# Two modulated linears around a 16-head per-token attention: softmax spreads ahead of the key turn, one key copy on ScalarE, stores a period later, another order in the fill

## The reference, cut to what matters

```python
def modulated_linear(x, s, aff_w, aff_b, w, b):
    style = s @ aff_w.T + aff_b
    w_mod = w[None, :, :] * style[:, None, :]
    demod = jax.lax.rsqrt(jnp.sum(w_mod * w_mod, axis=2) + EPS)
    ...
    return jnp.einsum('bni,boi->bno', x, w_mod) + b
...
x = x + L0(x)                       # modulated linear, clipped to +-256
kx = modulated_linear(x, ..., k_w)  # (B, N, 16 heads, 32)
scores = einsum('bnhd,bnjd->bnhj', kx, kx) / sqrt(32)
out = einsum('bnhj,bnjd->bnhd', softmax(scores), kx)
x = x + modulated_linear(out, ..., o_w)
```

## Time and profile before

| | us |
|---|---|
| median of 3 runs (760.2 to 765.8) | 765.31 |
| the profiled execution | 764.73 |
| its span in the profile | 762.9 |
| PE busy | 693.0 |
| DVE busy | 626.1 |
| ACT busy | 517.5 |
| POOL busy | 151.7 |

### The profile page before, as it was taken

How to read it: one execution, slowest core, us unless ns; L and a number is a source line. 1 busy time by engine, 2 the same in 40 slices (tenths; PEclk the granted TensorE clock), 3 DMA queues, 4 the chain that set the end, 5 groups by cost and what they waited for, 6 DMA issues and landing times.

```text
span 762.9 us, 21634 instructions
## 1 busy us (share of the span) xinstructions
PE 693.0 (91%) x8886; PEld 675.9 (89%) x8886; DVE 626.1 (82%) x1048; ACT 517.5 (68%) x1040; POOL 151.7 (20%) x139
## 2 busy tenths in 40 slices
PE   7999968999999999999999999999999899989896
PEld 6999968899888889988889998898999898889785
DVE  3689866998888898888899888889988888997662
ACT  4887855777667677666767766677767677765662
POOL 2024202222012222201222210222221122222200
PEclk9999999999999999999999999999999999989898
DMA  9267676467756676876567775657677665756853
GB/s 292 96 167 194 190 199 194 138 172 218 198 149 186 191 215 172 220 183 172 173 196 197 191 222 153 188 174 208 182 202 206 162 192 171 217 140 149 228 151 110
DMA packets 229666, 140.37 MB, mean 184 GB/s; under 512 B 141248, under 2 KB 223168, under 8 KB 229568
## 3 DMA queue, kind: packets, MB, share of 16 engines
q1 hardware_dynamic: 229568, 139.00, 65.0%
HBM read 71.85 MB, written 67.11 MB: 182 GB/s over the span
## 4 chain that ended last, share of the span: by engine, by line
DVE 53%; PE 22%; issue 9%; ACT 9%; DMA 4%; POOL 1%; SPq 1%; DVEq 0%; ACTq 0%; POOLq 0%
DVE p_bd L795 14%; PE y_ps L476 8%; PE lin_ps L413 7%; PE s_ps L458 6%; DVE o L773 5%; DVE x L754 5%; DVE v L744 4%; DVE x_lo L676 4%; DVE sc L759 3%; DVE x L752 3%; DVE sc L782 3%; DVE mx L764 3%; DVE p_turned L788 2%; DVE sc L766 2%; ACT sc L569 2%
## 5 line engine op out<-in xcount | busy, mean ns | idle before, releaser
L413 PE MATMUL lin_ps<-x_hi,w_hi 128*128 128x256 f32 x1008 | 287.3, 285 | 6.5 <-DVE w_lo L705 3.4
L413 PE MATMUL lin_ps<-x_lo,w_hi 128*128 128x256 f32 x1008 | 283.1, 281 | 0.0
L413 PE MATMUL lin_ps<-x_hi,w_lo 128*128 128x256 f32 x1008 | 282.9, 281 | 0.0
L383 POOL COPY k_bd<-k_rhs 32x1024 f32<-32x1024 f32 x128 | 147.4, 1151 | 568.1 <-DVE k_rhs L733 562.5
L413 PEld LDWEIGHTS lin_ps<-x_hi,w_hi 128*128 128x128 f32 x1008 | 191.3, 190 | 13.7 <-issue 13.5
L413 PEld LDWEIGHTS lin_ps<-x_lo,w_hi 128*128 128x128 f32 x1008 | 191.4, 190 | 0.2 <-issue 0.2
L413 PEld LDWEIGHTS lin_ps<-x_hi,w_lo 128*128 128x128 f32 x1008 | 191.3, 190 | 0.0
L413 PE MATMUL lin_ps<-y_hi,w_hi 128*128 128x256 f32 x528 | 150.4, 285 | 7.2 <-DVE y_lo L676 7.2
L413 PE MATMUL lin_ps<-y_lo,w_hi 128*128 128x256 f32 x528 | 149.3, 283 | 0.0
L413 PE MATMUL lin_ps<-y_hi,w_lo 128*128 128x256 f32 x528 | 149.2, 283 | 0.0
L509 ACT ACTIVATE x_hi<-x,style 128x256 fp32r<-128x256 f32 x252 | 113.0, 501 | 45.7 <-DVE x L754 39.4
(11 more groups left out here) (60 smaller groups left out, 727.1 us busy)
## 6 DMA issues: line engine op xcount, KB each, us to landing
x<-xT SPq DMA_DIRECT2D x32, 512.0 KB, 6.1
k_turned<-kx SPq DMA_DIRECT2D x32, 512.0 KB, 4.9
k_st<-k_turned SPq DMA_DIRECT2D x128, 128.0 KB, 3.1
v_turned<-k_rhs SPq DMA_DIRECT2D x32, 512.0 KB, 6.1
k_v<-v_turned SPq DMA_DIRECT2D x128, 128.0 KB, 3.2
y_turned<-y SPq DMA_DIRECT2D x128, 128.0 KB, 3.0
yr<-y_turned SPq DMA_DIRECT2D x32, 512.0 KB, 5.3
outT<-o SPq DMA_DIRECT2D x31, 512.0 KB, 4.0
```

The lines of the kernel that those rows point to most:

```text
L383: pool.tensor_copy(k_bd[HD * r:HD * (r + 1), r], k_rhs[HD * r:HD * (r + 1)]).then_inc(g_kbd, 1)
L413: mm = pe.matmul(lin_ps[:, n % NLB, 0:T], w[:, k, m * P:(m + 1) * P], r[:, k, :], start=(q == 0), stop=(q == len(passes) - 1))
```

## The change

On DVE in each period `spread_probabilities` comes ahead of `turn_k`, `turn_v` follows directly, and both `finish` come after `x_lo_of` of the next tile. POOL makes three of the four copies to `k_bd`; a new step `copy_keys` makes the fourth on ACT, behind `spread_some`. On SP `v_from_dram` is ahead of `y_to_dram`, and `store` is that of one tile earlier and stands between `y_to_dram` and `y_from_dram`. In the fill `scores` come sooner, `pv` later and in the middle of linears, with lists of ACT, DVE and SP to match. `WARM_L0` becomes 24. In the drain the lists get `copy_keys`, and the spreads of tile last-3 are ahead of the key turn of last-2.

```diff
-    WARM_STYLES, WARM_L0 = 9, 10
+    WARM_STYLES, WARM_L0 = 9, 24
+    POOL_GROUPS = 3
...
-            + blocks(K, 2) + blocks(L0, 4) + one("pv", 0) + one("scores", 1) + blocks(K, 3) + blocks(L0, 5)
-            + one("pv", 1) + one("scores", 2) + blocks(O, 0) + blocks(K, 4) + one("pv", 2) + one("scores", 3)
-            + blocks(O, 1) + blocks(K, 5) + one("pv", 3) + one("scores", 4))
+            + blocks(K, 2) + blocks(L0, 4) + one("scores", 1) + blocks(K, 3, [0, 1]) + one("pv", 0)
+            + blocks(K, 3, [2, 3]) + blocks(L0, 5, [0, 1]) + one("scores", 2) + blocks(L0, 5, [2, 3]) + one("pv", 1)
+            + blocks(K, 4) + one("scores", 3) + blocks(O, 0, [0, 1]) + one("pv", 2) + blocks(O, 0, [2, 3])
+            + blocks(K, 5) + one("scores", 4) + blocks(O, 1, [0, 1]) + one("pv", 3) + blocks(O, 1, [2, 3]))
...
             for i in range(FIRST_LOOP, last - 1):
                 k_to_dram(i - 1)
                 k_from_dram(i - 1)
+                v_from_dram(i - 2)
                 y_to_dram(i - 3)
-                v_from_dram(i - 2)
+                store(i - 5, 0, 1)
                 y_from_dram(i - 3)
                 load_x(i + 2)
                 v_to_dram(i - 1)
-                store(i - 4, 0, 1)
...
-                for r in range(R):
+                for r in range(POOL_GROUPS):
                     pool.tensor_copy(k_bd[HD * r:HD * (r + 1), r], k_rhs[HD * r:HD * (r + 1)]).then_inc(g_kbd, 1)
...
+            def copy_keys(c):
+                if c == 0:
+                    act.wait_ge(g_zero, 1)
+                act.wait_ge(v_krhs, c + 1)
+                for r in range(POOL_GROUPS, R):
+                    act.activation(k_bd[HD * r:HD * (r + 1), r], k_rhs[HD * r:HD * (r + 1)], ACT.Copy).then_inc(a_kbd, 1)
...
-                    (c0, x1_lo_of, 0), (c0, x1_lo_of, 1), (c1, turn_k), (c2, spread_probabilities), (c4, finish, 0),
-                    (c2, turn_v), (c4, finish, 1), (i + 1, x_lo_of, 0), (i + 1, x_lo_of, 1), (c3, y_lo_of, 0),
+                    (c0, x1_lo_of, 0), (c0, x1_lo_of, 1), (c2, spread_probabilities), (c1, turn_k), (c2, turn_v),
+                    (i + 1, x_lo_of, 0), (i + 1, x_lo_of, 1), (c4, finish, 0), (c4, finish, 1), (c3, y_lo_of, 0),
```

More of the change, by code:

```diff
@@ L305, in _ @@
             k_to_dram(2)
+            v_from_dram(1)
             k_from_dram(2)
-            v_from_dram(1)
             load_x(6)
             y_to_dram(0)
-            y_from_dram(0)
             v_to_dram(2)
             k_to_dram(3)
+            y_from_dram(0)
             k_from_dram(3)
@@ L316, in _ @@
             y_to_dram(1)
+            v_to_dram(3)
+            k_to_dram(4)
             y_from_dram(1)
-            v_to_dram(3)
-            store(0, 0, 1)
-            k_to_dram(4)
             k_from_dram(4)
@@ L323, in _ @@
             y_to_dram(2)
+            v_to_dram(4)
             y_from_dram(2)
-            v_to_dram(4)
-            store(1, 0, 1)
+            store(0, 0, 1)
             for i in range(FIRST_LOOP, last - 1):
@@ L334, in _ @@
                 v_to_dram(i - 1)
-                store(i - 4, 0, 1)
             k_to_dram(last - 2)
             k_from_dram(last - 2)
+            v_from_dram(last - 3)
             y_to_dram(last - 4)
-            v_from_dram(last - 3)
+            store(last - 6, 0, 1)
             y_from_dram(last - 4)
@@ L628, in _ @@
[L628 to L632, removed]
@@ L638, in _ @@
[L638 to L641, removed]
+                (1, k_out, 3), (O, roots), (2, x1_hi_of, 0), (2, x1_hi_of, 1), (0, copy_keys), (3, l0_out, 0),
+                (3, l0_out, 1), (3, l0_out, 2), (3, l0_out, 3), (4, x_hi_of, 0), (4, x_hi_of, 1), (0, even_scores),
@@ new lines, in _ @@
+                (2, k_out, 0), (0, exponentials), (2, k_out, 1), (2, k_out, 2), (2, k_out, 3), (1, copy_keys),
+                (3, x1_hi_of, 0), (4, l0_out, 0), (3, x1_hi_of, 1), (0, spread_some, 0), (4, l0_out, 1),
+                (0, spread_some, 1), (4, l0_out, 2), (0, spread_some, 2), (0, spread_some, 3), (4, l0_out, 3),
+                (5, x_hi_of, 0), (5, x_hi_of, 1), (1, even_scores), (3, k_out, 0), (1, exponentials), (3, k_out, 1),
+                (0, evacuate_y, 0), (0, evacuate_y, 1), (3, k_out, 2), (3, k_out, 3), (2, copy_keys),
@@ new lines, in _ @@
+                (4, x1_hi_of, 0), (4, x1_hi_of, 1), (1, spread_some, 0), (1, spread_some, 1), (5, l0_out, 0),
+                (1, spread_some, 2), (1, spread_some, 3), (5, l0_out, 1), (2, even_scores), (5, l0_out, 2),
+                (2, exponentials), (5, l0_out, 3), (6, x_hi_of, 0), (6, x_hi_of, 1), (3, copy_keys),
+                (1, evacuate_y, 0), (1, evacuate_y, 1), (4, k_out, 0), (0, y_hi_of, 0), (0, y_hi_of, 1),
+                (4, k_out, 1), (2, spread_some, 0), (2, spread_some, 1), (4, k_out, 2), (2, spread_some, 2),
@@ new lines, in _ @@
+                (2, spread_some, 3), (4, k_out, 3), (5, x1_hi_of, 0), (5, x1_hi_of, 1), (3, even_scores),
+                (0, o_out, 0), (3, exponentials), (0, o_out, 1), (2, evacuate_y, 0), (2, evacuate_y, 1),
+                (0, o_out, 2), (0, o_out, 3), (3, spread_some, 0), (3, spread_some, 1), (5, k_out, 0),
+                (3, spread_some, 2), (3, spread_some, 3), (5, k_out, 1), (4, copy_keys), (1, y_hi_of, 0),
+                (1, y_hi_of, 1), (5, k_out, 2), (5, k_out, 3), (1, o_out, 0), (1, o_out, 1), (3, evacuate_y, 0),
@@ new lines, in _ @@
+                (last - 4, y_hi_of, 1), (last - 1, k_out, 2), (last - 1, k_out, 3), (last, l0_out, 0),
+                (last, l0_out, 1), (last, l0_out, 2), (last, x1_hi_of, 0), (last, l0_out, 3), (last, x1_hi_of, 1),
+                (last - 3, evacuate_y, 0), (last - 3, evacuate_y, 1), (last - 2, even_scores), (last, k_out, 0),
+                (last - 2, exponentials), (last - 1, copy_keys), (last, k_out, 1), (last, k_out, 2), (last, k_out, 3),
+                (last - 5, o_out, 2), (last - 5, o_out, 3), (last - 3, y_hi_of, 0), (last - 3, y_hi_of, 1),
@@ new lines, in _ @@
+                (last - 2, spread_some, 0), (last - 2, spread_some, 1), (last - 2, spread_some, 2),
+                (last - 2, spread_some, 3), (last - 1, even_scores), (last - 4, o_out, 0), (last - 4, o_out, 1),
+                (last - 1, exponentials), (last, copy_keys), (last - 2, evacuate_y, 0), (last - 2, evacuate_y, 1),
+                (last - 4, o_out, 2), (last - 4, o_out, 3), (last - 1, spread_some, 0), (last - 1, spread_some, 1),
+                (last - 1, spread_some, 2), (last - 1, spread_some, 3), (last - 3, o_out, 0), (last, even_scores),
```

85 lines of the change are left out of this document (34 added, 51 removed).

## The result

The changed kernel takes 728.92 us (median of 4 runs, 728.44 to 729.27) against 764.4 of the kernel before (now 4 runs): a ratio of 0.9544, 95% interval 0.9505 to 0.9584. The forecast was 717 with a range of 708 to 738.

The account below looks back on a forecast made before the run. PE was to be the bound once its loop wait for DVE's transposed values went. Loop 36.0, start 1.4, fill 8.7 and drain 2.1 sum to 48.2 off 764.73, giving 717 us; range 708 to 738, own range 708 to 726.

Parts of the forecast that it names:

- The loop: Loop: PE's wait for the values goes, 0.1 us kept per period; 24 x 1.5 = 36.0 us gained.
- spreads without POOL: 1.66 for 4.01: DVE in the loop: the four softmax spreads, no longer under POOL's copies, save 2.35 us a period.
- Rival (c): Loop: spreads stay slow because POOL is not the cause; 721 us, its chance counted in the forecast's 0.66.
- Either half nearly does it: DVE in the loop: faster spreads alone leave no wait; moving the addition alone leaves 0.2 us.
- rival (a): Loop: the round trip through SP is the bound; 734 us at 21.8 a turn, 741 at 22.1; chance 0.20.
- The round trip: SP's queue in the loop: a turn of keys, values and y takes 20.6 us, under PE's 20.78; cost 0.
- (b): Loop: slower, every piece of the SP chain at its largest, 23.5 us a turn; 775 us, chance 0.03.
- The cover is used up: ACT in the loop: with the 1.05 us copy it finishes y just when scores end; further delay makes softmax late.
- rival (d): Loop: ACT's even scores come 1 to 2 us late, costing 0 to 0.5 a period; up to 729, chance 0.08.
- The fill: Fill: removed waits and slow-clock losses outweigh new waits of 4.8 us; 8.7 us gained, bounds 3 and 14.0.
- The start: Ahead of the first linear: more dummy matmuls keep PE's clock at full speed; 1.4 us gained, bounds 0 and 1.4.
- The drain: Drain: shorter waits for x_lo and the last key copies, less 0.7 for copy_keys; net 2.1 us, bounds 0 and 5.8.

Follow-up runs that it names:

- e1: The kernel before with only the softmax spreads put ahead of the key turn in the loop's DVE list; 723.80 us, ratio 0.950.
- e2: The kernel before with only both residual additions moved behind the low parts of the next tile in the loop's DVE list; 737.41 us, ratio 0.967.
- e3: The kernel before with the whole new DVE order of the loop and nothing else; 731.80 us, ratio 0.959.
- e7: The changed kernel with SP's old order in the loop; 729.33 us, ratio 0.956.
- e4: The changed kernel with all four key copies on POOL again; 723.29 us, ratio 0.947.
- e12: The kernel before with the loop's spreads ahead of the key turn and one of four key copies on ACT; 720.52 us, ratio 0.946.
- e5: The changed kernel with 10 instead of 24 dummy matmuls ahead of the first linear; 728.53 us, ratio 0.955.
- e11: The changed kernel with the key turn of tile 0 back at its old place in the fill's DVE list and four key copies on POOL; 718.87 us, ratio 0.943.

## Why the prediction was right, and where it was off

**The loop was the gain**: right in mechanism, 33.4 us for 36.0. The "spreads without POOL: 1.66 for 4.01" came out at 1.67, the transposes directly behind, the wait for `v` gone in every period, and e1 shows it with one exchange of two steps. Rival (c) is ruled out by the 1.67. (Its own working, 0.1 us more in 24 periods, gives 719.4 and not 721.)

**"Either half nearly does it"**: half right. The spreads alone do it (e1). The additions alone leave 0.2 of wait for `v`, as computed, but the sum stopped there: with SP's old order and four copies on POOL the round trip becomes late (e2, e3). That resembles rival (a), met in another kernel than I gave it for; that the held-back store does it is not shown, since e7 holds it back too.

**The round trip "taken: 0"** held: `yr` lands in 4.8 ("near 5"), kx in 2.9, ACT waits 5.6 us for it in 480, and SP's old order gives the same time (e7). Rivals (a) and (b) didn't come about. (The aside on a turn with both lone transfers at 3.2 us gives 19.1 and not 18.9, which changes nothing.)

**"The cover is used up"**: the cover was gone, and this is the term of the loop that was set at nothing. The copy took the 1.06 that was taken, and `even_scores` started 0.8 us later than before against the scores' end, somewhat less than the 1 to 2 of rival (d). Its price came on paths that I didn't name: the transposes ended 15.8 after the start of L0 (forecast 14.7) and `pv` started at 17.5, so it never waited, but the banks of O and K were emptied late and K's blocks grew by 0.15 a period against e1. That is 3.5 us in 23 periods and covers the 2.6 by which the loop missed; without the copy (e4) the loop gains 4.0. The copy does this only together with other parts of the change, since e12 has it at no cost.

**The fill is the step that failed.** 8.7 became 0.7 (1.3 less the start's 0.6), outside its bounds of 3 and 14. "The first three `pv` find their operands ready" was right, and so was the wait of `y_lo` (1.20 for about 1); the new wait of the `scores` of tile 4 came, with 1.49 for 3.8. Missing were two waits ahead of them: 2.99 for `x_lo` of tile 3 and 3.22 for the keys of tile 3. Both were in the lists. The layout followed the steps in PE's new order and took the steps that were moved *forward* on DVE, ACT and SP as free; `turn_k(0)` was one of them, and its effect through POOL is the one that I had just used for the loop. The scores of tile 3 were moved forward on PE as those of tile 4 were, and only the latter were checked against their keys. Behind the second the clock is half (scores in 3.64 us for 1.93), which the bound of 3 had foreseen in kind, at too high a floor.

**The start** gave 0.6 for 1.4 in this pair of profiles and 2.1 in the mean of all fourteen, so the term is neither confirmed nor refuted in size. Its mechanism is seen: the clock is 1.00 from 12 to 16 us. "The dummies end near 11.7" was a little early, the first linear follows them at 11.99, and the kernel before was shown at one of its faster starts. The medians tell nothing of it (e5).

**The drain** gave 0.9 for 2.1. The wait of the last `scores` is 1.1 (forecast: 3.7 less 1.2) and that of `x_lo` 0.8. The term that was too small is `copy_keys`, "0.7 at most that PE sees": `pv` waits 2.0 and 2.5 us for spreads that ACT makes late (above), and e4, without the copy, has a drain shorter by 5.9.

Together: 2.6 short in the loop, 8.8 in start and fill, 1.2 in the drain, 12.6 of 48.2. The 728.92 lies outside the forecast's own range, 708 to 726, and next to the 729 that rival (d) was given, though (d) was to act through `pv` and did not. The time lay in the range of 708 to 738 because the high end of that took in rival (a), which did not come about. That is luck; the fill's bounds don't account for it.

## What to carry to other kernels

Before reordering a whole kernel, find the one pair of steps whose exchange takes an engine out of another's shadow and time that alone; here it gave all of the gain, and of the edits beside it two (the key turn of the fill, the copy on ACT) took 9 or 10 us back (e11). A step that is moved ahead is as much a cost as one moved back: follow what it sets off on other engines (here POOL's copies) and who runs under that. An engine whose slack is used up can be late without its first reader waiting; look for the wait where the buffers come free. Where a wait is put down to nothing, compare its end with the ends of all operands: the drain's stop of 2.0 us was ACT's last spread.

## What the runs showed of the hardware

DVE and POOL slow each other by amounts that depend on the operation. The copy of POOL that begins at 43.98 under a DVE instruction takes 1.88 us where the next takes 1.12. Under POOL's copies of 32 x 1024 the clip of `x` (L763) takes 1.27 us for the 0.43 that it takes alone in the loop, an addition of 128 x 512 takes 1.40 for 0.69, four `x_lo` take 3.19 for 1.66 (the last of them behind POOL), and two value transposes keep their 1.29. Taken one by one the affected instructions go in step with POOL's copies. In the period of the earlier trace rows three of the four spreads take 1.26 each, where 1.66 was the price of all four; the copies take 1.12 to 1.23, and the spreads that begin at 409.63 and 410.81 end at 410.89 and 412.07, 0.28 behind the copies that end at 410.61 and 411.79. After the change two `x_lo` take 1.25 each and end 0.28 behind a copy as well. So in these rows each affected DVE instruction that runs into a copy lasts about as long as a copy, however short it is alone. The Trainium skill, "SBUF — State Buffer", section "Who interferes with whom", has DVE and GpSimd exclude each other on a shared port pair; the rows of the additions and of `x_lo` agree with that, and two transposes, 1.29 with POOL done and 1.29 under it, don't show it.

ACT copies 32 x 1024 in 1.06 us, and 128 x 1024 took 1.05 before: with as many columns, a quarter of the partitions buys nothing.

PE once stood 0.8 us in the loop, inside a block of matmuls (at 275.1 us), for nothing that the profile shows. That stop makes one period of 21.8 in the changed kernel; e5 has three, of 1.0 to 1.5 us, and e1 none. The cause stays open. The stops ahead of `pv` in the drain are not of this kind: each ends 0.10 us after ACT's last spread.
